# Adding the experts' results of tiles 4 to 15 to x by accumulating transfers

## What is computed

```
x = x + xattn0(layernorm(x), ctx)       # 16 heads, 77 keys of each batch row
x = x + moe(layernorm(x))               # 8 experts, top 2 of a softmax router, and a shared expert
x = x + xattn1(layernorm(x), ctx)       # as the first, other weights, a mask for each batch row
x = x + ffn(layernorm(x))               # fake-quantised (int8 activations, ternary weights) 256-1024-256, GELU
```

## Time and profile before

| what | us |
|---|---|
| median of three executions | 992.73 (986.76 to 996.06) |
| the profiled execution | 997.49 |
| its span, first to last instruction | 995.3 |
| barrier at the end of the expert stage | 568.3 |
| barrier at the end of the second attention | 817.2 |

### The profile page before, as it was taken

How to read it: one execution, slowest core, us unless ns; L and a number is a source line. 1 busy time by engine, 2 the same in 40 slices (tenths; PEclk the granted TensorE clock), 3 DMA queues, 4 the chain that set the end, 5 groups by cost and what they waited for, 6 DMA issues and landing times. The chain is left out here.

```text
span 995.3 us, 23601 instructions
## 1 busy us (share of the span) xinstructions
PE 840.9 (84%) x9005; PEld 667.3 (67%) x9020; DVE 749.3 (75%) x1668; ACT 603.4 (61%) x1124; POOL 560.6 (56%) x691
## 2 busy tenths in 40 slices
PE   5799999997688884988887587998999869999995
PEld 5587788786577674777776565776777745555553
DVE  3688888786566765666676378887889858999996
ACT  2466777664444432655555044765666648999995
POOL 2445767553055453355666396779989964433330
PEclk9799999999799995999899778999999979999997
DMA  8491999100021123455552483500000000000000
GB/s 247 68 347 48 368 390 400 43 2 2 6 86 73 68 85 110 141 169 174 165 164 100 143 253 51 87 3 2 2 2 3 2 1 12 27 28 27 27 28 26
DMA packets 49599, 99.04 MB, mean 100 GB/s; under 512 B 10065, under 2 KB 32209, under 8 KB 49489
## 3 DMA queue, kind: packets, MB, share of 16 engines
q1 hardware_dynamic: 36224, 71.79, 21.2%
q0 software_dynamic: 11648, 25.18, 8.3%
q10 hardware_dynamic: 1616, 0.58, 0.4%
HBM read 36.71 MB, written 60.82 MB: 98 GB/s over the span
## 5 line engine op out<-in xcount | busy, mean ns | idle before, releaser
L557 POOL TENSOR_TENSOR sm_a<-sm_a,mx_a 128x616 f32<-128x616 f32 x128 | 157.5, 1230 | 113.3 <-DVE mx_a L874 112.9
L798 ACT ACTIVATE pr_a<-sm_a 128x616 f32<-128x616 f32 x128 | 91.5, 715 | 102.3 <-POOL sm_a L557 102.3
L1141 POOL DMA_INDIRECT mixed<-rep,qidx_f x92 | 90.5, 984 | 78.0 <-DVE rep L1641 53.3
L867 DVE TENSOR_TENSOR sm_a<-pS_a,mask 128x616 f32<-128x616 f32 x128 | 100.7, 790 | 23.8 <-PE pS_a L708 23.7
L1135 POOL DMA_INDIRECT slots<-sx,idx_f x64 | 65.1, 1017 | 80.6 <-DVE idx_f L1534 63.5
L723 PE MATMUL pT_a<-ident,pr_a 128*128 128x128 f32 x640 | 98.3, 284 | 7.8 <-ACT pr_a L798 3.4
L874 DVE TENSOR_REDUCE mx_a<-sm_a 128x8 f32<-128x616 f32 x128 | 99.0, 773 | 0.0
L746 PE MATMUL pO_a<-aw,ot_a 128*128 128x256 f32 x256 | 75.2, 418 | 24.4 <-DVE ot_a L895 23.8
L723 PEld LDWEIGHTS pT_a<-ident,pr_a 128*128 128x128 f32 x640 | 71.9, 143 | 23.7 <-issue 14.2
L697 PE MATMUL pA_a<-sx,aw 128*128 128x128 f32 x512 | 72.6, 288 | 0.9 <-ACT sx L792 0.9
L746 PEld LDWEIGHTS pO_a<-aw,ot_a 128*128 128x128 f32 x256 | 45.1, 196 | 41.6 <-DVE ot_a L895 37.9
(11 more groups left out here) (307 smaller groups left out, 2433.0 us busy)
## 6 DMA issues: line engine op xcount, KB each, us to landing
slots<-sx SPq DMA_DIRECT2D x16, 2176.0 KB, 8.9
sx<-slots SPq DMA_DIRECT2D x23, 544.0 KB
x<-x_in SPq DMA_DIRECT2D x4, 1024.0 KB, 11.2
x<-mixed POOLq DMA_DIRECT2D x4, 1024.0 KB, 9.9
out_x<-x SPq DMA_DIRECT2D x32, 128.0 KB, 1.7
rep<-gu_in SPq DMA_DIRECT2D x10, 256.0 KB, 4.7
aw<-aw_in SPq DMA_DIRECT2D x2, 1024.0 KB, 7.1
ha<-mixed SPq DMA_DIRECT2D x2, 1024.0 KB, 7.1
```

The lines of the kernel that those rows point to most:

```text
L557: pool.tensor_tensor(heads, heads, mx[u][:, g, :].rearrange("p (h a) -> p h a", a=1).broadcast_to([P, HG, SK]), ALU.subtract).then_inc(shi ...
L798: act.activation(pr[u][:, g, 0:NS], sm[u][:, g, :], ACT.Exp).then_inc(exped, 1)
L867: dve.tensor_tensor(sm[u][:, g, :].rearrange("p (b h k) -> p b h k", b=ROWS_OF_HEADS, k=SK), pS[:, :, g * QS:(g + 1) * QS].rearrange("p b ...
L1141: pool.indirect_dma_start(dram["mixed"][:], bass.IndirectOffsetOnAxis(qidx[:, at:at + 1], 0), ys[q % 2][:, j, :], None).then_inc(out_moved ...
```

## The change

Tiles 4 to 15 are added to x as tiles 16 to 31 were: `fetch` takes b = 0 (there tiles 4 to 7 alone, 0.5 MB) and b = 1 (tiles 8 to 15, 1 MB). The first choices of both are issued by GpSimd at the end of the expert stage, after a wait for all scatters. The second choices are issued in the second attention: b = 0 right after GpSimd's memsets, b = 1 after `second_pair` in step -3. The loads to `rep` and `ha`, the functions `second_half` and `join` and their semaphores are gone. `early_stats` waits for `got[1][0]` in step -1 and for `got[1][1]` from step 0 on.

```diff
 def fetch(pool, dram, sb, b, a):
+    first = ST if b == 0 else b * TB
+    many = (b + 1) * TB - first
     if a > 0:
         pool.wait_ge(sb["got"][a - 1][b], 16)
-    pool.dma_start(sb["x"][:, b * TB:(b + 1) * TB, :], mixed_rows(dram, a, b * TB, TB),
+    pool.dma_start(sb["x"][:, first:first + many, :], mixed_rows(dram, a, first, many),
                    accum_op=ALU.add).then_inc(sb["got"][a][b], 16)
...
                 rows = lambda ap: ap.rearrange("(k p) n -> p k n", p=P)
-                for a in range(TOPK):
-                    sp.dma_start(yb[a], mixed_rows(dram, a, TB, TB)).then_inc(y_in, 16)
                 for name in ("w1", "w2"):
...
             pool.memset(powers[:], -0.5).then_inc(powers_ok, 1)
+            if layer == 1:
+                fetch(pool, dram, sb, 0, 1)
...
-            def join(n, a):
...
-                pool.tensor_tensor(X[:, own, :], X[:, own, :], yb[a][:, 2 * n:2 * (n + 1), :], ALU.add).then_inc(joined, 1)
...
-            def second_half(a):
...
-                pool.tensor_tensor(of, of, sb["rep"][a][:, 0:ST * D], ALU.add).then_inc(first_joined, 1)
...
             def between(t):
-                if t in JOINS:
-                    join(JOINS.index(t), 0)
...
             def behind(t):
-                if t in JOINS:
-                    join(JOINS.index(t), 1)
...
                 if layer == 1 and t == -3:
                     second_pair()
-                    second_half(0)
-                if layer == 1 and t == -2:
-                    second_half(1)
+                    fetch(pool, dram, sb, 1, 1)
...
                 if layer == 1 and t == 0 and j == 0:
-                    act.wait_ge(first_joined, ST - AHEAD + 1 + TOPK)
+                    act.wait_ge(first_joined, ST - AHEAD + 1)
...
                     for n in normed_at(t):
-                        if n == 0:
-                            act.wait_ge(joined, ST * TOPK)
...
-                elif b == 0:
-                    dve.wait_ge(first_joined, ST - AHEAD + 1 + (TOPK if t == -1 else 0))
-                elif b == 1:
-                    dve.wait_ge(joined, TOPK * (t // 2 + 1))
-                elif b > 1:
+                elif t == -3:
+                    dve.wait_ge(first_joined, ST - AHEAD + 1)
+                else:
                     dve.wait_ge(sb["got"][TOPK - 1][b], 16)
...
                              mixed_rows(dram, 1, AHEAD + n, 1)).then_inc(sb["y_in"][1], 16)
-            for a in range(TOPK):
-                sp.dma_start(ys[a], mixed_rows(dram, a, ST, ST)).then_inc(sb["y_in"][2], 16)
...
                     pool.sem_inc(ys_free, 1)
+            pool.wait_ge(out_moved[(NQ - 1) % 2], 16 * ST * ((NQ + 1) // 2))
+            fetch(pool, dram, sb, 0, 0)
+            fetch(pool, dram, sb, 1, 0)
```

More of the change, by code:

```diff
@@ L468, in attention_phase @@
         spare_half = lambda t: pT[:, (J * (t - 3) + J - 1) % 2, D:2 * D]
-        joined = sem("joined")
         if layer == 1:
-            s_m, s_abs, s_tot, s_q, s_clip, y_in = (sem(n) for n in (
-                "first_step", "abs_sums", "abs_total", "quant_step", "clipped", "y_in"))
+            s_m, s_abs, s_tot, s_q, s_clip = (sem(n) for n in (
+                "first_step", "abs_sums", "abs_total", "quant_step", "clipped"))
             s_scaled = sem("scaled")
@@ L475, in attention_phase @@
             halves = [slice(i * HID, (i + 1) * HID) for i in range(2)]
-            yb = [sb["ha"][:, a * TB:(a + 1) * TB, :] for a in range(TOPK)]
             raw = [sb[n][:].rearrange("p k n -> p (k n)") for n in ("w1", "w2")]
@@ L480, in attention_phase @@
             SCALES, CLIPS, ROUNDS = (24, 25, 28, 29), (26, 27, 30, 31), (27, 28, 31, 32)
-            UNITS, ROUND_X, JOINS = (24, 25, 26, 27), (28, 29), (-1, 1, 3, 5)
+            UNITS, ROUND_X = (24, 25, 26, 27), (28, 29)
         block = ctx.enter_context(nc.Block())
@@ L2036, in build @@
         sb["sx"] = [ctx.enter_context(nc.sbuf_tensor(f"sx{i}", [P, ST, ROW], F32)) for i in range(2)]
-        sb["y_in"] = [ctx.enter_context(nc.semaphore(f"first_in{n}")) for n in range(3)]
+        sb["y_in"] = [ctx.enter_context(nc.semaphore(f"first_in{n}")) for n in range(2)]
         attention_weights(ctx, 1)
```

## The result

The changed kernel takes 1003.81 us (median of 4, 1002.5 to 1007.26) against 992.03 of the kernel before (986.76 to 996.06): ratio 1.0113, 95% interval 1.0079 to 1.0147. It is slower, by some 12 us; 993.1 was forecast and 1002 was the upper end of its range. The profiled execution took 1004.79 us, with a span of 1002.9.

What follows compares the result with a forecast made beforehand. Bound: a tile handed round the engines in 32 steps, transfers playing no part. Opening +0.35, step 0 +1.3, step 1 -1.25, rest 0, sum +0.4 us on the median 992.73: 993.1 us, range 986 to 1002.

Steps and rivals of the forecast that it cites:

- The end of the expert stage: Two first-choice transfers issued by GpSimd there, hidden under VectorE's and TensorE's key and value work: priced at 0.
- Rival 2: Expert stage's end: GpSimd's drain counts from the new landing, barrier 7.5 us late, 1000.6 us; chance 0.21.
- The opening: Second attention's start to step -1: statistics of tiles 4 to 7 slightly later, +0.35 us (between -0.3 and +2).
- A: GpSimd's second-choice transfer of tiles 4 to 7, in the second attention's opening; landing predicted between 575 and 579, middle 577.
- B: GpSimd's second-choice transfer of tiles 8 to 15, issued from 573.7; landing predicted between 583.3 and 590, taken as 587.
- Step 0: Second attention: VectorE's statistics of tile 8 wait for all of B; +1.3 us, between -0.65 and +4.2.
- rival 3: Second attention: B lands last and TensorE's clock falls in the gap; +6.3, 999.0 us; chance 0.10.
- Step 1: Second attention: VectorE's mask conversion ends earlier without GpSimd's addition of tiles 10 and 11; -1.25 us, between 0 and -2.9.
- The clock: TensorE's dip at 602 to 604 may go, another may come at 587; set against each other at 0, each bounded by 3 us.

Runs made afterwards that it cites:

- the loads behind B: The changed kernel, but SyncE loads w1, w2 and the six rows only after second choices of tiles 8 to 15 landed: 1000.29 us, ratio 1.005.

## Why the prediction was wrong

**The end of the expert stage (predicted 0, measured +6.2).** This is the step that failed first. I had seen the 12.2 us drain and had both counts, from the issue and from the landing, and took the one that costs nothing. All eleven profiles fit a later-of-two: the drain ends 8.7 us after GpSimd's last instruction or wait, or some 4.4 us after the landing of its last direct transfer, whichever is later. The kernel before could show only the first: it issues no direct transfer there, and its last scatter had moved its data by 554.0, 7.7 us ahead of the drain's end. The cost is what stands out past VectorE's end: 6.2 us for 1.5 MB in the changed kernel (5.9 and 9.0 in two versions of it), 3.2 for 0.5, nothing for 1 MB of plain loads. Rival 2 had the place and the sign. That its size was near (7.5) is in part luck: it let the drain run 7.1 us past the landing where 4.4 were measured, and had the landing 0.4 us past VectorE's end where it came 1.8 past it.

**The opening (predicted +0.35, measured +2.3).** GpSimd's issue of A put the statistics of tiles 2 and 3 off by 1.3 us (1.7 predicted). With A landed these would have hidden, as they do with the loads behind B, where the statistics of tiles 4 to 7 start 9.95 us after VectorE's first instruction of the stage, against 10.05 before. But A took 11.5 us to land and not 8. The mis-sized term is its time beside SyncE's loads: I bounded it at twice the 3.2 us of data, and counted from 2.6 us behind the issue to the landing it took nearly three times (8.9 us). With the loads held back A landed 6.3 us after its issue.

**Step 0 (predicted +1.3, measured +4.9 from step 0's first reduction to step 1's).** The sum of all transfers was right: 21 us were predicted, and the DMA engines were busy from 573.3 to 594.2. The middle between the two ends was wrong. B was last of all to land, as in rival 3, and 1.5 us past the late bound: 22.5 us after A's issue, where the bound had 21. That "nothing in the trace shows accumulations and loads side by side" was no reason for the middle.

**Step 1 (predicted -1.25, measured -2.0).** The size of the gain was near, its reason half right. With only the addition moved the conversion shrank by 1.23 us, the predicted 1.25, and again ended 0.35 us behind GpSimd's last instruction. But that brought step 2 no earlier. With only the transfer moved the conversion shrank by 2.24 and step 2 came 1.8 us earlier: without that transfer the three GpSimd instructions in a row do not keep VectorE out. So the removed addition, on which the term rests, was not shown to be worth anything, and that the number was near is luck.

**The clock (predicted 0).** Both sides that were set against each other are in the traces. The dip behind step 1's conversion is gone: TensorE was granted 0.52 at 602 to 604 before, and 1.00 from 600 to 620 after. Behind the idle time that the wait for B left on TensorE there is a new one, 0.50 from 597 to 599. Another, 0.50 from 587 to 592, is not B's doing, since it is there with the loads behind B too (588 to 594), where nothing is waited for. Between steps 2 and 6 is the place where 1.6 us were won. The profile before has two stretches of some 3.5 us at about 0.5 there, the one after has one. Whether that is the 1.6 us is open: the kernel with the addition moved also has only one such stretch there, and took 30.1 us between the two reductions, against 30.6 before and 29.1 in the changed kernel.

**The range.** The rivals were priced one by one. The drain and the late landings are separate losses and were both there: together they give 13.5 us by step 0, and only the 3.6 won back kept the total at 10 to 12. The prediction did name the pair, with 0.11 for "rival 2 with a late B or a dip", and added its bounds up to +16.7; but it then put the upper end of the range at 1002, which leaves that pair out. The end should have stood where rivals 2 and 3 come together (992.73 + 6.3 + 7.5 = 1006.5).

## What to carry to other kernels

A transfer issued by GpSimd just ahead of a barrier isn't free because nobody waits for its semaphore: in these runs the engine's drain ended some 4.4 us after its landing, so the landing and that much more have to lie ahead of the last engine's end. Work taken off an engine and given to the DMA engines has to be priced with all that runs on these at that hour, and with the late end of the landing where the first consumer is near; loads that nobody needs yet are better held back (one wait on SyncE's queue was worth 6.5 us here). Risks with separate causes add up; a range that takes them one at a time is too narrow.

## What the hardware showed that I had not expected

- GpSimd's drain with no direct transfer ahead of it ends 8.7 to 8.8 us after GpSimd's last instruction or wait (six profiles). Behind direct transfers it ends 4.3 to 4.5 us after the last landing (five profiles): at 569.9 with a landing at 565.6, at 572.1 with 567.7, and at 569.0 with plain loads landed at 564.5.
- An accumulating transfer into SBUF of 1 MB fills all DMA engines for 6.3 us, where plain loads of 5.9 MB took 18: about half the rate. Beside loads it fell behind: 18.5 us to landing against 9.5.
- A mask conversion of VectorE beside three GpSimd instructions takes 1.10 us, but 3.3 (three profiles) if GpSimd has issued a 1 MB transfer some 4 us before. Why was not tried.
